# Weight half blocks split during attention: one split held for a row normalization, its stores and loads issued behind the loads of x

## What is computed

```
x = x + tanh(g_xattn) * attention(layernorm(x), ctx)       # 8 heads of 64, Wq, Wk, Wv, Wo, bo
x = x + tanh(g_ffn)   * ffn(layernorm(x))                  # 8 experts, all rows through all of them
    h = gelu(x @ w1[e] + b1[e]);  y = h @ w2[e] + b2[e];  out = sum over e of y * norm_g
```

## Time and profile before

| | us |
|---|---|
| runs of before (three) | 1816.6, 1818.35, 1818.82; median 1818.35 |
| the profiled execution, its own time | 1820.77 |
| its span, first to last instruction | 1819.0 |
| mean granted TensorE clock in it | 0.994 of full speed |
| PE busy / DVE / POOL / ACT | 1773.9 / 1454.3 / 1360.4 / 942.8 |

### The profile page before, as it was taken

One profiled execution on the slowest core, in us unless ns is written; L12 is line 12 of the kernel. 1 busy time (PEld: TensorE's weight loads), 2 busy tenths in 40 slices (PEclk: granted clock), 3 DMA queues, 4 the chain that ended last, 5 costly groups with the idle time before them and its releaser, 6 DMA issues.

```text
span 1819.0 us, 35778 instructions
## 1 busy us (share of the span) xinstructions
PE 1773.9 (98%) x9780; PEld 1625.5 (89%) x9780; DVE 1454.3 (80%) x2532; ACT 942.8 (52%) x1832; POOL 1360.4 (75%) x1334
## 2 busy tenths in 40 slices
PE   7899999999999999999999999999999999999998
PEld 7799998999989978899899889888899999999997
DVE  7688878888888884776777677667988989989987
ACT  6577676767667764343443444343444444444443
POOL 5677676767667568778777777757989889889863
PEclk9899999999999999999999999999999999999999
DMA  5233434233332335433533533544343443433422
GB/s 181 80 101 96 116 89 127 77 109 100 95 99 82 111 109 198 172 127 147 187 127 115 191 152 118 187 177 151 141 157 116 144 145 126 144 135 132 148 105 93
DMA packets 120065, 236.78 MB, mean 130 GB/s; under 512 B 14392, under 2 KB 91192, under 8 KB 111808
## 3 DMA queue, kind: packets, MB, share of 16 engines
q1 hardware_dynamic: 120000, 235.99, 38.9%
HBM read 166.24 MB, written 69.73 MB: 130 GB/s over the span
## 4 chain that ended last, share of the span: by engine, by line
PE 85%; DVE 6%; issue 5%; DMA 1%; POOL 1%; SPq 1%; ACT 1%; POOLq 0%; DVEq 0%; ACTq 0%
PE scores L1014 29%; PE bank L1084 19%; PE bank L871 14%; PE bank L1055 10%; PE bank L952 4%; PE scores L942 4%; PE bank L964 3%; DMA xa<-in_x 1%; DVE xa L1255 1%; DVE acc_t L1488 1%; DVE queries L1323 1%; DVE stats L1245 1%; PE scores L1177 0%; PE bank L878 0%; POOL probs L1927 0%
## 5 line engine op out<-in xcount | busy, mean ns | idle before, releaser
L1014 PE MATMUL scores<-xs,w1s 128*128 128x448 f32 x2646 | 576.2, 366 | 3.4 <-ACT h_sum L1664 2.6
L1014 PEld LDWEIGHTS scores<-xs,w1s 128*128 128x128 f32 x2646 | 494.5, 188 | 51.3 <-ACT h_sum L1664 8.1
L1488 DVE TENSOR_TENSOR acc_t<-bank,acc_t 128x448 f32<-128x448 f32 x608 | 351.7, 615 | 18.8 <-PE bank L1084 18.8
L1417 DVE TENSOR_TENSOR h_sum<-scores,h_sum 128x448 f32<-128x448 f32 x189 | 117.0, 619 | 126.2 <-ACT h_sum L1664 55.5
L1664 ACT ACTIVATE h_sum<-scores 128x448 f32<-128x448 f32 x189 | 101.9, 539 | 222.7 <-PE scores L1014 222.6
L1055 PE MATMUL bank<-w2s,hs 128*128 128x512 f32 x798 | 190.6, 393 | 1.0 <-DVE xres L1377 1.0
L2160 POOL TENSOR_TENSOR hs<-h_full,hs 128x448 fp32r<-128x448 f32 x132 | 154.0, 1171 | 47.3 <-ACT hs L1823 47.2
L1055 PEld LDWEIGHTS bank<-w2s,hs 128*128 128x128 f32 x798 | 149.9, 189 | 31.2 <-issue 1.5
L1927 POOL TENSOR_SCALAR probs<-probs,row_inv 112x750 f32<-112x750 f32 x60 | 130.7, 2179 | 50.0 <-DVE row_inv L1348 49.9
L1822 ACT ACTIVATE h_full<-h_sum,b1T 128x448 f32<-128x448 f32 x149 | 99.3, 667 | 129.4 <-DVE h_sum L1417 99.3
L871 PE MATMUL bank<-wv,ctxT 128*125 128x256 f32 x1152 | 152.3, 284 | 3.6 <-DVE keys L1259 3.6
(11 more groups left out here) (184 smaller groups left out, 3669.6 us busy)
## 6 DMA issues: line engine op xcount, KB each, us to landing
w1s<-w_scratch SPq DMA_DIRECT2D x46, 1792.0 KB, 7.4
w_stage<-in_L_ffn_w SPq DMA_DIRECT2D x82, 512.0 KB, 3.6
w_scratch<-w1s SPq DMA_DIRECT2D x18, 1792.0 KB, 6.1
w_scratch<-w2s SPq DMA_DIRECT2D x28, 896.0 KB, 5.3
ctx_raw<-in_ctx SPq DMA_DIRECT2D x16, 376.0 KB, 3.2
ctx_raw<-in_ctx SPq DMA_DIRECT2D x14, 374.0 KB, 3.2
xa<-in_x SPq DMA_DIRECT2D x16, 224.0 KB, 4.3
w_stage<-in_L_ffn_w SPq DMA_DIRECT2D x14, 256.0 KB, 5.2
```

Of the source, the lines that this page charges most:

```text
L1014: mm = pe.matmul(product_bank(g, name)[:, 0:TH], w1s[j % 2][:, s, W_OF[name], kc, :], xs[:, i, m, kc, :], start=opens and n == 0, stop=n == 5,
L1417: dve.tensor_tensor(h_sum[:, q, :], product_bank(g, product)[:, 0:TH], h_sum[:, other, :], ALU.add).then_inc(sum_out, 1)
L1488: dve.tensor_tensor(home, bank, home, ALU.add).then_inc(z_added, 1)
```

## The change

POOL: in the middle batches E1 first waits until `ln_out` counts A<1.0 of this batch (the first half's normalized rows are written). In batch 0 there is no such wait, and E1 stands in front of D1 rather than behind it. E0, E2 and E3 are as before, and so is the work of every split.

SP: in all batches but the last, the store of split 1 and the load of split 3 are issued behind both `load_x` and not in front of `store_yT`. In batch 0 the store of split 0 and the load of split 2 are moved behind `load_x` as well.

```diff
--- before.py
+++ after.py
@@ -237,7 +237,7 @@
     FIRST = {eng: [i for i in items if i[1] >= 0] for eng, items in BODY_PLAN.items()}
 
     early_pool = [i for i in FIRST["pool"] if i != ("E", 0, 1)]
-    d1 = early_pool.index(("D", 0, 1)) + 1
+    d1 = early_pool.index(("D", 0, 1))
     FIRST["pool"] = early_pool[:d1] + [("E", 0, 1)] + early_pool[d1:]
 
     bank_of = {
@@ -778,15 +778,12 @@
                         load_xres(b, qt)
                 else:
                     store_x2(b - 1, 0)
-                if name != "last":
+                if name == "middle":
                     store_ahead(b, 0)
                     load_ahead(b, 2)
                 if name != "first":
                     store_x2(b - 1, 1)
                     load_xres_next(b)
-                if name != "last":
-                    store_ahead(b, 1)
-                    load_ahead(b, 3)
                 for qt in range(2):
                     if name != "first":
                         store_yT(b - 1, qt)
@@ -800,7 +797,12 @@
                         sp.wait_ge(in_psum["X"], number(("X", 0, qt), b))
                         alone(sp, passed["sp"])
                         load_x(b + 1, qt)
+                if name == "first":
+                    store_ahead(b, 0)
+                    load_ahead(b, 2)
                 if name != "last":
+                    store_ahead(b, 1)
+                    load_ahead(b, 3)
                     load_ctx(b + 1, 1)
 
             batches(sp, batch)
@@ -1969,6 +1971,9 @@
                     pool.tensor_tensor(ctxT[:, 1, c, k0:k1], ctx_raw[:, c, 0:k1 - k0],
                                        ctxT[:, 0, c, k0:k1].bitcast(F32), ALU.subtract).then_inc(lo_out["C"], 1)
                 elif kind == "E":
+                    if item[2] == 1 and not (isinstance(b, int) and b == 0):
+                        pool.wait_ge(ln_out, n_ln(1, b - 1, 0))
+                        alone(pool, passed["pool"])
                     split_ahead(b, item[2])
                 elif kind == "L":
                     which, qt = item[2:]
```

## The result

The changed kernel takes 1799.63 us, the median of four runs (1798.62 to 1804.57), against 1818.59 for the kernel before on the same occasion: 0.9894 of it, 95% interval 0.9862 to 0.9926. Six further runs beside the kernel before gave 0.9906 (0.9889 to 0.9924). The forecast was 1800.2, range 1796 to 1808.

A forecast was written before the change was run, and what follows sets the result against it. PE was taken to bound the kernel, busy 1773.9 of 1819.0 us, so only its waits could yield time. Batch 0's -10.55 and the middle batches' -7.6 gave -18.1: 1802.6 profiled, less 2.42 for a median of 1800.2, range 1796 to 1808.

The forecast's parts named there:

- Batch 0, SP and clock: Batch 0: earlier x loads remove PE's 8.89 us wait before T3.0, and 1.66 of half clock goes too: -10.55.
- The clock term: Batch 0 after T3.0: without the wait PE keeps full clock, saving 1.66 us, from comparing batch 0 with batch 2.
- Batch 0, POOL: Batch 0: E1 pauses for split 0's store; M3.1, ending at 62.4, has 2.3 us to spare before T3.0.
- Middle batches, the wait: Middle batches: A<1.0 takes 0.53, E1 restarts 0.3 behind it, T2.0 comes 1.31 us earlier per batch.
- The second rival: Middle batches: E1 restarts 1.3 us later than forecast, only x's earlier loads gain: 1806.5 us; chance 0.11.
- The third rival: Middle batches: A<1.0 is slow for a reason of its own, T2.0 0.8 later at worst: 1812.6 us; chance 0.03.
- Middle batches, SP: Middle batches: x comes about 4 us earlier, ending the 0.66 wait that makes batches 3 to 6 0.33 longer.
- Sum: Whole kernel: -10.55 in batch 0 and -7.6 in six middle batches make -18.1 us, a median of 1800.2.

The follow-up runs named there:

- the second profile of before: The kernel before, unchanged, profiled once more in a single run: 1818.04 us.
- the first experiment: The changed kernel's new order of SP alone, with POOL as in the kernel before: 1809.03 us, ratio 0.9933.
- the two pauses: The changed kernel without E1's wait for A<1.0; E1 instead waits for its own second and third instructions, leaving two pauses on POOL: 1795.4 us, ratio 0.9868.
- E1 behind M2.1: The changed kernel with E1 moved behind M2.1 in POOL's plan and no wait for A<1.0: 1795.72 us, ratio 0.9859.
- the order that gained most: The changed kernel with M2.1 in front of L<1.1 on POOL and E1 behind L<1.1, waiting for A<1.1: 1794.09 us, ratio 0.9854; once more, 1796.41.
- the one late pause: The changed kernel without E1's wait for A<1.0, with one pause behind E1's fourth instruction: single run, 1799.24 us.

## Why the prediction was right

*Batch 0, SP and clock.* Forecast -10.55, measured -10.89 (-11.13 against the second profile of before). T3.0 was put at about 64.6 and came at 64.72. The clock term, 1.66, was read from one comparison and came as 43.88 - (106.75 - 64.72) = 1.85.

*Batch 0, POOL.* E1's pause before its third instruction was to be 2.3 and was 2.6; M3.1 was to end at 62.4 and ended at 62.0. That it would have been 0.6 late with E1 behind D1 was shown by the first experiment: 0.8.

*Middle batches, the wait.* A batch was to take 78.67 and took 78.65 on average. T2.0 was put 1.31 earlier and came 1.20 earlier (27.14 to 25.94), since POOL restarted 0.44 behind A<1.0, not 0.3; the wait that remained, "about 1 us" and M2.1's, was 0.96. The second rival needed a restart 1.3 us later than those 0.3; it was 0.14 later. The third rival, A<1.0 slow for its own reasons, falls with its 0.54 beside an idle POOL, and with the two pauses. Batch 1 loses 0.2 to 0.4: the prediction's words have it gain nothing, its sum counts it at 78.67 like the others, and the sum was right.

*Middle batches, SP.* The reading was half right. The wait for x did go, and alone it was worth 0.4 in batches 3 to 6 against one profile of before and 0.2 against the other. That it makes batches 3 to 6 longer than batch 2 fits: in the first profile DVE waited 0.7 for x in batches 2 and 6, which took 79.9 to 80.0, and 1.0 to 1.2 in batches 3 to 5, which took 80.3 to 80.6; with SP's order alone batches 3 to 6 (79.90) are no longer than batch 2 (79.93). But it isn't a separate term: with POOL's change alone it cost next to nothing too, because SP's queue moved up with A<1.1.

*Sum.* -18.1 forecast; -18.6 in the parts that the change touches, -19.0 between the medians of the day. The profiled executions differ by 21.5; the 3 us above are mostly two stretches at half clock in the profile of before. Against the second profile of before the same parts give -17.7. The median came within 0.6 us, partly by luck: the kernel before had medians of 1818.35 to 1821.36 on different occasions, the changed one 1799.63 and 1803.16.

## What to carry to other kernels

When a short VectorE operation is several times longer in one place than elsewhere, see what GpSimd does in that moment: a small gap in its stream, or another order of its list, can be enough, and costs less than a wait that delays everything queued behind. After freeing a queue, ask which item on it is now the last to arrive, and try the list with the urgent one in front: here that was worth another 1.2 us a batch, 0.9 of which E1 behind M2.1 gave already. Then see where the same two engines meet next: the order that gained most made another VectorE operation 2.5 us longer in batch 7. And removing part of a wait of TensorE may bring less than it promises: the stretch at half clock can then move from idle time onto work.

## What the runs showed of the hardware that was not expected

- In batches 2 to 6, A<1.0 ran to its end 0.28 us after the first gap in POOL's stream, in two kernels, after 2.64 and 1.24 us. Beside the scaling of 2.18 us it had no gap and ended 1.16 to 1.17 us behind the scaling's start, whether it had begun 0.04 or 0.55 behind it. What decides between the two kinds of POOL instruction stays open. So does batch 1: in the kernel before, in both its profiles, and with the one late pause, A<1.0 took 0.82 there beside E1 without any gap, and E1's fourth instruction was stretched to 0.64; with SP's order alone it took 2.66. In all of these E1's third instruction began within 0.05 us of A<1.0, so that distance doesn't decide it. DVE and POOL in batch 1 of the kernel before:

```profile
134.19 0.82 DVE L1255 TENSOR_SCALAR xa<-xres,mean_var,rstd 112x512 f32<-112x512 f32 x1
```
```profile
134.23 0.50 POOL L2011 CAST w2s<-ahead_second 128x384 fp32r<-128x384 f32 x1
134.70 0.64 POOL L2013 TENSOR_TENSOR w_stage<-w_stage,ahead_second 128x128 f32<-128x128 f32 x1
```

- The granted clock fell to 0.50 during an idle stretch of PE, but not at a fixed point of it. In the kernel before PE was idle from 64.75 and the clock fell at 67.2; in its second profile PE was idle from 65.16 and it fell at 68.5; with POOL's change alone PE was idle from 64.74 and it fell at 69.8. Around waits of 1.0 us it stayed at 1.00 in most places, though not in all: in batch 7 of the first profile of before it fell at 650.9, behind two such waits that ended at 643.2 and 648.4, and in the changed kernel, with waits of 1.1 and 1.0 us that ended at 624.8 and 629.9, it did not fall. On one occasion the changed kernel gave 1798.96 us at a mean clock of 1.000 and 1806.84 at 0.996. Such stretches come and go between executions of the same kernel and cost more than many a change; a difference of 3 us between two single profiles says nothing until they are found and set aside.
